# Layer 1's linear attention on one core: full-array products of a step side by side, and another PSUM bank for the state update's fourth pair

## What is computed

```python
Q = (x @ Wq + bq).reshape(Bsz, Tlen, H, dh)      # K, V alike
Qp, Kp = relu(Q), relu(K)
Qc, Qs = Qp * cosw, Qp * sinw                    # Kc, Ks alike
def step(carry, inp):                            # over the tokens
    S_cos = S_cos + kc[..., :, None] * v[..., None, :]
    S_sin = S_sin + ks_[..., :, None] * v[..., None, :]
    z_cos, z_sin = z_cos + kc, z_sin + ks_
    num = einsum('bhi,bhij->bhj', qc, S_cos) + einsum('bhi,bhij->bhj', qs, S_sin)
    den = maximum(sum(qc * z_cos + qs * z_sin, axis=-1), 1e-06)[..., None]
    return (S_cos, S_sin, z_cos, z_sin), num / den
out = out @ Wo + bo                              # then x + gate * out
```

## Time and profile before

| | |
|---|---|
| runs | 871.23, 871.64, 872.01 us; median 871.64 us |
| the profiled execution | its span is 873.5 us, from the first to the last instruction, with no time of its own beside it: 1.9 us above the median |
| busy, share of the span | PE 94%, PEld 81%, DVE 70%, ACT 49%, POOL 45% |
| the chain that ended last | PE 78%, DVE 7%, issue 5%, POOL 4%, ACT 3%, DMA 2% |
| layer 1's attention (64 steps) | from about 298 us to about 779 us |

### The profile page before, as it was taken

How to read it: one execution, slowest core, us unless ns; L and a number is a source line. 1 busy time by engine, 2 the same in 40 slices (tenths; PEclk the granted TensorE clock), 3 DMA queues, 4 the chain that set the end, 5 groups by cost and what they waited for, 6 DMA issues and landing times.

```text
span 873.5 us, 32577 instructions
## 1 busy us (share of the span) xinstructions
PE 817.3 (94%) x13678; PEld 704.8 (81%) x13678; DVE 614.8 (70%) x1775; ACT 432.0 (49%) x944; POOL 394.9 (45%) x399
## 2 busy tenths in 40 slices
PE   6999985699997899999999999999999999999998
PEld 5777854588996688888888888888888888878887
DVE  7888885575664775675777785876876776858875
ACT  6556532544343755555556465565564464433322
POOL 4358877224454653644545654457442342500000
PEclk9999995599998999999999999999999999999999
DMA  9714100524322100000100100100000000027761
GB/s 292 252 63 160 37 26 11 175 76 128 94 76 84 31 27 4 27 3 3 51 3 3 29 3 3 53 3 4 4 3 3 5 3 3 4 57 148 157 125 40
DMA packets 67905, 49.66 MB, mean 57 GB/s; under 512 B 5298, under 2 KB 62785, under 8 KB 67377
## 3 DMA queue, kind: packets, MB, share of 16 engines
q1 hardware_dynamic: 64288, 42.41, 18.1%
q0 software_dynamic: 3328, 5.16, 1.8%
q10 hardware_dynamic: 144, 0.02, 0.0%
HBM read 33.20 MB, written 16.10 MB: 56 GB/s over the span
## 4 chain that ended last, share of the span: by engine, by line
PE 78%; DVE 7%; issue 5%; POOL 4%; ACT 3%; DMA 2%; SPq 0%; ACTq 0%; POOLq 0%; DVEq 0%
PE psum L1531 11%; PE psum L1636 8%; PE psum L1663 7%; PE psum L1614 7%; PE psum L2294 5%; PE psum L1217 5%; PE psum L1566 5%; PE psum L1595 5%; PE psum L2312 4%; PE psum L1651 3%; PE psum L1577 3%; PE psum L1549 3%; PE psum L1252 3%; POOL disp L307 3%; DMA sb_e_x<-disp 1%
## 5 line engine op out<-in xcount | busy, mean ns | idle before, releaser
L2192 POOL TENSOR_TENSOR sb_a_qr<-sb_h,sb_a_csq 128x512 f32<-128x512 f32 x64 | 81.4, 1294 | 113.8 <-PE psum L1636 107.9
L2192 POOL TENSOR_TENSOR sb_a_qr<-sb_a_qp,sb_a_csq 128x512 f32<-128x512 f32 (+1 forms) x64 | 72.2, 1151 | 116.4 <-PE psum L1636 116.4
L1531 PE MATMUL psum<-sb_wkv,sb_a_hs 128*128 128x512 f32 x384 | 122.5, 428 | 1.0 <-ACT sb_a_hs L1982 0.7
L1790 ACT ACTIVATE sb_a_vr<-sb_a_va,sb_consts 128x520 f32<-128x520 f32 x128 | 86.4, 725 | 5.0 <-DVE sb_a_va L2052 4.3
L307 POOL DMA_INDIRECT disp<-sb_h,sb_slot x64 | 67.8, 1060 | 25.5 <-issue 17.6
L1531 PEld LDWEIGHTS psum<-sb_wkv,sb_a_hs 128*128 128x128 f32 x384 | 63.8, 191 | 13.0 <-ACT sb_a_hs L1982 0.9
L1636 PE MATMUL psum<-sb_a_vr,sb_a_kb 64*64 64x130 f32 x1920 | 72.7, 277 | 1.6 <-issue 1.6
L2073 DVE TENSOR_TENSOR sb_a_mid<-psum,sb_a_state 128x130 f32<-128x130 f32 x112 | 47.4, 424 | 36.2 <-PE psum L1636 36.1
L1163 POOL DMA_INDIRECT chosen<-sb_m_h3t,sb_e_row x40 | 39.4, 985 | 70.9 <-ACTq L1331 55.2
L1614 PE MATMUL psum<-sb_a_mid,sb_a_qr 64*64 64x65 f32 x2048 | 70.7, 218 | 0.0
L1217 PE MATMUL psum<-sb_e_xt,sb_e_ws 128*128 128x320 f32 x384 | 64.8, 324 | 4.5 <-DVE sb_e_hs L1411 3.7
(11 more groups left out here) (283 smaller groups left out, 1947.4 us busy)
## 6 DMA issues: line engine op xcount, KB each, us to landing
sb_h<-turned SPq DMA_DIRECT2D x32, 256.0 KB, 5.5
sb_e_w<-in_w SPq DMA_DIRECT2D x24, 256.0 KB, 3.2
chosen<-sb_empty SPq DMA_DIRECT2D x8, 512.0 KB, 6.3
sb_a_g<-chosen SPq DMA_DIRECT2D x12, 256.0 KB, 3.5
disp<-sb_empty SPq DMA_DIRECT2D x4, 650.0 KB, 9.9
sb_e_x<-disp SPq DMA_DIRECT2D x7, 325.0 KB, 5.4
sb_a_wo<-in_wo SPq DMA_DIRECT2D x4, 512.0 KB, 4.8
out<-sb_x SPq DMA_DIRECT2D x7, 256.0 KB, 4.0
```

Of the source, the lines that this page charges most:

```text
L1531: ins = pe.matmul(self.values_bank(i) if kv else self.bank[0], hs[:, part, at:at + P], self.Wkv[ws][:, h, w], start=(k == 0), stop=(k == 2))
L1790: ins = act.activation(self.Vr[i % 2][:, :, k, :], self.Va[i % 3][:], ACT.Copy, scale=self.c[("cos1", "sin1")[k]][:, n:n + 1])
L2192: ins = g.tensor_tensor(self.Qr[i % 2][:, k, :, t], qp, rows(self.csQ[:, k, c * P + t.start:(c + 1) * P], PH), ALU.mult)
```

## The change

In words:

- The output product of tile n moves from step 2n+2 (between inter and update) to step 2n+3, behind the turned outputs and ahead of the turned keys. It writes the last 128 columns of bank 4 instead of bank 1. Only the last tile's keeps its place behind the loop.
- The logits of group m move along, to step 8m+15, into bank 5; group 6's from behind the loop to step 63.
- A normed group is turned behind the keys' product at the start of a step. The two norms change places: the first norm's statistics, roots and normed tiles come at i % 8 = 4, 5, 6 and are turned at 7, the second's at 2, 3, 4 and are turned at 5.
- The update's fourth pair goes to bank 1 from update 2 on. The update then waits for `c_KTc` (the copy of the turned keys), no longer for `c_Sm`; intra still waits for `c_Sm`.
- Inter waits in those steps for `c_x` and `c_lg` (x added, logits copied).
- Half of the turned outputs have a second buffer, so that a tile's product can run one step later.
- On DVE the addition of x (and the logits' copy) moves from behind the scores to between the state's three pairs and the values.

```diff
     def update_tensor(self, i):
-        pe.wait_ge(S["c_Sm"], max(0, i))
+        if i < 2:
+            pe.wait_ge(S["c_Sm"], i)
+        else:
+            pe.wait_ge(S["c_KTc"], i + 1)
...
-                bk, at = (6 + r, j * 130) if j < 3 else (3, r * 130)
+                home, at = (self.bank[6 + r], j * 130) if j < 3 else (self.fourth_home(i), r * 130)
...
+    OUTPUT_AT = {2 * n + 3: n for n in range(NT - 1)}
+    LOGITS_AT = {8 * m + 15: m for m in range(NGRP - 1)}
+    def output_home(self, n):
+        return self.bank[1][:, 0:D] if n == NT - 1 else self.bank[4][:, 512 - D:512]
+    def logits_home(self, m):
+        return self.bank[1][:, D:D + G4 * E1] if m == NGRP - 1 else self.bank[5][:, 512 - G4 * E1:512]
+    def fourth_home(self, i):
+        return self.bank[3 if i < 2 else 1]
...
     def inter_tensor(self, i):
         pe.wait_ge(S["c_state"], 2 * i + 2)
+        if i in self.OUTPUT_AT:
+            pe.wait_ge(S["c_x"], self.OUTPUT_AT[i] + 1)
+        if i in self.LOGITS_AT:
+            pe.wait_ge(S["c_lg"], self.LOGITS_AT[i] + 1)
...
     def outputs_turned(self, i):
         pe.wait_ge(S["c_On"], i + 1)
-        pe.wait_ge(S["c_state"], min(4 * NT, 2 * i + 3))
+        if i == 0:
+            pe.wait_ge(S["c_state"], 3)
...
     def l1_tensor(self):
+            if i % 8 == 5 and i >= 8:
+                self.tiles_turned(self.xn1, "c_xn3", i // 8 - 1, [("c_state", 2 * i + 1)])
+            if i % 8 == 7 and i // 8 + 2 < NGRP:
+                self.tiles_turned(self.xn1, "c_xn1", i // 8 + 2, [("c_state", 2 * i + 1)])
...
                 self.outputs_turned(i - 1)
+            if i in self.OUTPUT_AT:
+                self.output1_tensor(self.OUTPUT_AT[i])
+            if i in self.LOGITS_AT:
+                self.logits_tensor(self.LOGITS_AT[i], [])
...
     def l1_vector(self):
-            if i >= 0 and i % 8 == 2 and i // 8 + 2 < NGRP:
-                parts = self.stats_parts(i // 8 + 2, self.st1, "1", ("c_mix", 5 * (i // 8) + 15))
-            if i >= 8 and i % 8 == 4:
+            if i >= 8 and i % 8 == 2:
                 some(parts, 30)
                 parts = self.stats_parts(i // 8 - 1, self.st3, "3", ("c_x", 4 * (i // 8)))
+            if i % 8 == 4 and i // 8 + 2 < NGRP:
+                some(parts, 30)
+                parts = self.stats_parts(i // 8 + 2, self.st1, "1", ("c_mix", 5 * (i // 8) + 15))
...
                 self.state_three(i)
+            if i in self.OUTPUT_AT:
+                self.output1_vector(self.OUTPUT_AT[i])
+            if i in self.LOGITS_AT:
+                self.logits_vector(self.LOGITS_AT[i])
...
-            if i >= 2 and i % 2 == 0:
-                self.output1_vector((i - 2) // 2)
...
     def outputs_scalar(self, i):
-        act.wait_ge(S["c_Y"], i // 2)
-        out, got = self.oT1[:, PH * h:PH * (h + 1), :], self.bank[3].rearrange("p (m t) -> p m t", t=P)
+        act.wait_ge(S["c_Y"], max(0, i // 2 - 1 + h))
+        out, got = self.oT1[h][i // 2 % 2], self.bank[3].rearrange("p (m t) -> p m t", t=P)
...
     def moe_tensor(self):
-        self.logits_tensor(NGRP - 2, [("c_h3", NGRP - 1)])
-        self.output1_tensor(NT - 1, [])
+        self.output1_tensor(NT - 1)
```

More of the change, by code:

```diff
@@ L1473, in l1_buffers @@
         self.O = sb("a_o", [P, 2, PH, DH])
-        self.oT1 = sb("a_ot", [P, HD // P, P])
+        halves = sb("a_ot", [P, HD // P, P])
+        spare = self.h3T[:, (NT - G4) * P:].rearrange("p (m t) -> p m t", t=P)
+        self.oT1 = [[halves[:, 0:PH, :], spare], [halves[:, PH:, :]] * 2]
         self.hT1 = sb("a_ht", [P, G4 * P])
@@ L1590, in scores_tensor @@
         pe.wait_ge(S["c_OTc"], i)
+        if i == 0:
+            pe.wait_ge(S["c_state"], 1)
         for j in range(PH):
@@ L1708, in l1_tensor @@
             self.first_queries(1, j)
-        bank1 = [("c_KTc", 1)]
         for i in range(steps):
@@ L1718, in l1_tensor @@
                 self.outputs_turned(i - 1)
+            if i in self.OUTPUT_AT:
+                self.output1_tensor(self.OUTPUT_AT[i])
+            if i in self.LOGITS_AT:
+                self.logits_tensor(self.LOGITS_AT[i], [])
             if known(i + 1):
-                self.keys_turned1(i + 1, bank1)
-                bank1 = [("c_KTc", i + 2)]
+                if i == 0:
+                    read = [("c_KTc", 1)]
+                elif i == 1:
+                    read = [("c_h1", 3), ("c_hl", 3)]
+                else:
+                    read = [("c_state", 2 * i + 1)]
+                if i % 8 == 5 and i >= 8:
+                    read = [("c_h3", i // 8)]
+                if i % 8 == 7 and i // 8 + 2 < NGRP:
+                    read = [("c_h1", i // 8 + 4)]
+                self.keys_turned1(i + 1, read)
             if known(i + 2):
@@ L1729, in l1_tensor @@
                 self.hidden_product(0, 4, 0)
-            if known(i):
-                self.scores_tensor(i)
-                self.inter_tensor(i)
-            if i == 0 or (i % 8 == 5 and i // 8 + 2 < NGRP):
-                m = i // 8 + 2 if i else 1
-                self.tiles_turned(self.xn1, "c_xn1", m, bank1)
-                bank1 = [("c_h1", m + 2)]
-            if known(i) and i % 8 == 7 and i >= 8:
-                m = i // 8 - 1
-                self.tiles_turned(self.xn1, "c_xn3", m, bank1)
-                bank1 = [("c_h3", m + 1)]
-            if i >= 2 and i % 2 == 0:
-                n, logits = (i - 2) // 2, []
-                if i % 8 == 0 and i >= 16:
-                    self.logits_tensor(i // 8 - 2, bank1)
-                    bank1, logits = [], [("c_lg", i // 8 - 1)]
-                self.output1_tensor(n, bank1)
-                bank1 = [("c_x", n + 1)] + logits
+            self.scores_tensor(i)
+            self.inter_tensor(i)
+            if i == 0:
+                self.tiles_turned(self.xn1, "c_xn1", 1, [("c_KTc", 2)])
             if known(i + 1):
                 self.update_tensor(i + 1)
-            if known(i):
-                self.intra_tensor(i)
+            self.intra_tensor(i)
             if i < 8:
@@ L1843, in l1_scalar @@
                 self.values_rotated(i + 1)
+            if i % 8 == 5 and i >= 8:
+                self.tiles_scaled3(i // 8 - 1)
+            if i % 8 == 7 and i // 8 + 2 < NGRP:
+                self.tiles_scaled1(i // 8 + 2)
             if 1 <= i <= 8:
@@ L2103, in output1_vector @@
         v.wait_ge(S["c_xb"], n // G4 + 1)
-        v.tensor_tensor(x, self.bank[1][:, 0:D], x, ALU.add).then_inc(S["c_x"], 1)
+        v.tensor_tensor(x, self.output_home(n), x, ALU.add).then_inc(S["c_x"], 1)
     def logits_vector(self, m):
@@ L2108, in logits_vector @@
         v.wait_ge(S["c_lgmm"], m + 1)
-        v.wait_ge(S["c_Y"], min(NT, 4 * m + 8))
-        v.tensor_copy(self.lg1[:, m % 2, :, :].rearrange("p n e -> p (n e)"),
-                      self.bank[1][:, D:D + G4 * E1]
+        v.tensor_copy(self.lg1[:, m % 2, :, :].rearrange("p n e -> p (n e)"), self.logits_home(m)
                       ).then_inc(S["c_lg"], 1)
@@ L2168, in l1_vector @@
                 some(weights, 4)
-            if i >= 2 and i % 2 == 0:
-                self.output1_vector((i - 2) // 2)
             if i % 8 == 0 and i >= 16:
                 some(weights, 30)
-                self.logits_vector(i // 8 - 2)
             some(parts, 2)
@@ L2228, in l1_gpsimd @@
                 self.bias_added(1)
[L2229 removed]
+            if i % 8 == 3 and i >= 8:
+                self.roots(i // 8 - 1, self.rt3, "3")
+            if i % 8 == 5 and i // 8 + 2 < NGRP:
                 self.roots(i // 8 + 2, self.rt1, "1")
[L2231 to L2233 removed]
+            if i % 8 == 7 and i // 8 + 2 < NGRP:
+                self.low_part(g, i // 8 + 2)
                 self.bias_added(i // 8 + 2)
[L2235 to L2236 removed]
             if i in (25, 41):
```

31 lines of the change are left out of this document (10 added, 21 removed).

## The result

| | before | changed |
|---|---|---|
| nine runs each, median (lowest to highest) | 871.64 us (870.82 to 873.33) | 869.67 us (867.95 to 873.11) |
| span of the profiled execution | 873.5 us | 866.6 us |
| scores of step 0 to scores of step 63 ("the stage" below) | 476.6 us | 474.1 us |

The ratio is 0.9975 (95% interval 0.9964 to 0.9985): 2.0 us less, where I forecast 7.7 us less, 863.9 us, with a range from 860.5 to 869.0. The measured time, 869.67, lies above the range.

The account below looks back on a forecast made before the run. PE's own list was taken to be the stage's time. The terms -6.2 - 2.85 - 3.1 + 1.35 + 3.1 gave -7.7 us, so 871.6 became 863.9 us, with a range from 860.5 to 869.0.

Parts of the forecast that it names:

- Part 1: Between inter and update in 31 even steps: moving the output product away saves 0.20 us each, 6.2 us less.
- Part 2: Update in 19 odd steps with nothing between: no longer waiting for `c_Sm` saves 0.15 us each, 2.85 us less.
- Part 3: Normed groups turned in 12 steps, moved behind the keys' product: 0.26 us less each, 3.1 us less.
- Part 4: Work coming ahead of the scores of step 63: a turned group 0.44, group 6's logits 0.91, together 1.35 us more.
- Part 5: DVE's list in shortened even steps: PE stalls 0.43 us in five steps and 0.95 in step 58, 3.1 us more.
- Part 6: New waits, inter for x and the update for the keys' copy `c_KTc`: both cost nothing.
- the first rival: DVE's weights pieces in six short steps held while POOL runs: 5.5 us more, 869.4 us; chance 0.13.

Follow-up runs that it names:

- The run with bank 3: The changed kernel with the update's fourth pair back in bank 3, waiting for the masked scores again, new product order kept: ratio 1.020 to the kernel before.
- the kernels with fewer stops: The changed kernel with 48 idle products in PE's idle time and 13 between inter and update: 0.990; the same with three weights pieces in step 58: 0.9905.

## Why the prediction was wrong, step by step

- **Part 1, output product**: right in kind, too small. From 2.13 us to 0.04 and 1.79 it is 0.30 a step, 9.4 us (unrounded) and not 6.2. I priced a product at 0.118 in both places; among its like it takes 0.112, and its row went from 2.05 to 1.95 us. The size of the intervals around it (0.11 and 0.09) held.
- **Part 2, the wait for `c_Sm`**: 0.15 x 19 held. Not foreseen: each update's row became 0.05 us shorter, 1.12 to 1.07, 3.1 us over 62. The run with bank 3 has the 0.05 back, so it belongs to the bank.
- **Part 3, normed groups**: 0.35 us behind the keys' product (450.56 to 450.91 in step 20) and not 0.44, so 0.35 x 12 = 4.2 us less, not 3.1.
- **Part 4, step 63**: 0.35 + 0.81 = 1.16 us against 1.35. The wait of the first down product for DVE grew from 0.6 to 2.1 us, as forecast: what was freed behind those scores is idle time.
- **Part 5, DVE**: twice too large. Step 58 took 1.25 us (forecast 0.95), and the first rival's mechanism is what did it: L2481 was held. In the five other steps it was 0.2 us in one (42), and 0.2 in up to four of them in the kernels with fewer stops. Together about 1.5 us more, not 3.1.
- **Part 6, new waits**: nothing, right. In no run does inter wait for x or the update for ACT.
- These parts sum to about -17; the trace has -16.2 in the stage less stops. So the sum, set against a kernel without the supply, was wrong by a factor of two, on the safe side.
- **The step that failed** is the one ahead of them all: "PE's own list is the time of this stage, and a gain has to come out of what PE's timeline shows between its products". I took for granted that PE gets its list at any rate. No term and no rival had the supply. It cost 13.7 us: the stops went from 2.4 to 16.1. The signs stood in the profile of before: three stops of 0.45 to 1.17 us inside the update of steps 15, 31 and 47, with no releaser but "issue", exactly 16 steps apart and in the densest part of the list. I didn't look for gaps inside groups, since I read each group as one row.
- **The base** was off too: I took the profiled span for a time and put it 1.9 above the median. It was 3.2 above, which doesn't enter the sum against the median but would have spoilt any reading of the two spans.

That the two errors partly cancelled (an undersized gain, a missing cost) is why the time lay only 5.8 us from the forecast, and the mechanism that I gave for it would still have been wrong.

## What to carry to other kernels

Ask of a dense stretch of small products not only what each costs but how many instructions it issues: where PE stood at a border here, 3.5 us in the median had gone by since the border before, and mostly 3.0 to 4.0 (late packets left out), and 64x64 products of 65 columns use 256 instructions up in 2.3. A gap without a releaser inside a group, at record numbers that are multiples of 256 apart, is that. Taking a slow full-array product out of such a stretch can give back what the product had hidden. The measured pair (2.4 and 16.1 us) is for one place of the borders; an estimate over all places, from the two profiles' starts without the stops and 3.3 us from border to border, gives 4.5 us in the mean for the list before and 15 for the changed one, late packets not counted. With those in, the list before did worse (52.4 us of stops with 28 idle products, 43.7 in the changed one). Where the borders fall is a property of all instructions ahead, so before believing a small gain or loss, shift the list by some tens of idle instructions and time it again: here the same kernel ran from 0.990 to 1.040 of the kernel before by that alone.

## What the runs showed that I had not expected

- PE's instructions come in packets of 16384 bytes while the kernel runs, 109 of them. At the stops a packet mostly began 0.5 to 1.6 us after a border, 1.0 in the median; it took 0.9 to 1.5, and its first instruction ran 2.2 to 2.9 us after it began, 2.5 in the median.
- Sometimes a packet begins late, 3 to 5.5 us after the border, with nothing else moving. With borders in intra of the odd steps this came in step after step and made about 35 us of the 57 that 28 idle products cost the kernel before. It comes behind stops in even steps too: behind those of steps 18, 34 and 50 of the changed kernel (3.06, 4.48 and 4.36 us). Its cause is open.
- The order of the products by itself is worth 1.0 us of the stage less stops, and the bank of the fourth pair on top of it 15.2 us.
- A TENSOR_TENSOR on DVE with both operands in SBUF takes 0.22 us, and 1.11 when POOL's row began 0.25 earlier: POOL's row is two instructions, the first of which ended at 734.80, and the one on DVE ended at 734.88. The Trainium skill (SBUF — State Buffer, Terms) says that VectorE and GpSimd take a shared pair of ports by turns; the trace agrees.
